# A sparse graph-attention layer: fewer count operations on VectorE, the edge one-hot scaled on ScalarE, the first search ahead of the arrival count's load

## What is computed

```python
h = relu(layernorm(x))
e = leaky_relu(h @ a[:256] + (h @ a[256:]).T, 0.2)      # 8192 x 8192
U = softmax(where(adj > 0, e, -9e15), axis=1)
prop = U @ h
rowsum = sum(U * 0.5 * U, axis=1)
feat = soft_threshold((1 - coe[2]) * h + prop - h * rowsum, 1e-6)
pu = U @ feat
feat_odd2 = coe[0] * (feat - coe[3] * pu) + (1 - coe[0]) * h0
feat_even2 = pu + (feat - coe[3] * pu) * rowsum
out = x + coe[1] * feat_even2 + (1 - coe[1]) * feat_odd2
```

## Time and profile before

| | us |
|---|---|
| median of 3 runs | 1553.82 |
| lowest and highest | 1546.98, 1554.12 |
| the profiled execution's own time | 1548.79 |
| its span | 1547.2 |

### The profile page before, as it was taken

The page is one execution under the profiler, slowest core; times in us unless marked ns, Lnnn a source line. Parts: engine busy times, 40 slices in busy tenths (PEclk is TensorE's granted clock), DMA queues, the critical chain, the costliest instruction groups (busy, mean ns, idle before and its releaser), DMA issues. The chain is left out here.

```text
span 1547.2 us, 27877 instructions
## 1 busy us (share of the span) xinstructions
PE 941.7 (61%) x3386; PEld 548.0 (35%) x3449; DVE 994.3 (64%) x5594; ACT 840.0 (54%) x1754; POOL 587.9 (38%) x642
## 2 busy tenths in 40 slices
PE   0013567687767666766766766767552555666676
PEld 0001124444444333333333333333331444544443
DVE  5882555787788788788788788788772112233444
ACT  2371456788777778777777777777422222111111
POOL 2000434534333233222122112112115777777776
PEclk9965568878888889888787777777655777788979
DMA  4974579889999999999999999988314556677887
GB/s 92 345 261 195 207 256 384 305 305 365 349 351 356 350 345 358 343 339 350 339 334 345 342 329 346 339 322 317 147 56 138 145 162 189 186 217 217 244 249 222
DMA packets 151067, 427.18 MB, mean 276 GB/s; under 512 B 30123, under 2 KB 112697, under 8 KB 134516
## 3 DMA queue, kind: packets, MB, share of 16 engines
q1 hardware_dynamic: 120872, 348.93, 61.0%
q0 software_dynamic: 30160, 77.90, 17.2%
HBM read 401.29 MB, written 33.85 MB: 281 GB/s over the span
## 5 line engine op out<-in xcount | busy, mean ns | idle before, releaser
L293 ACT ACTIVATE SG<-W,ABOVE 128x4096 bf16<-128x4096 f32 x126 | 467.0, 3706 | 120.0 <-DVE cnt L891 117.6
L586 POOL DMA_INDIRECT R<-haug_d,IDS x228 | 228.9, 1004 | 711.7 <-issue 711.7
L305 PE MATMUL TP<-SG,FOLD 128*128 128x512 bf16 x1006 | 315.3, 457 | 68.0 <-ACT SG L293 63.8
L628 ACT ACTIVATE DG<-ident,WSR 128x128 f32<-128x128 f32 x228 | 75.0, 391 | 311.3 <-PE ACC L642 284.9
L637 PE MATMUL ACC<-R,DG 128*128 128x256 f32 x538 | 193.1, 510 | 0.0
L1504 DVE SCALAR_TENSOR_TENSOR W<-ACC,SELF,W 128x256 f32<-128x256 f32 x63 | 30.5, 484 | 243.8 <-PE ACC L642 243.6
L305 PEld LDWEIGHTS TP<-SG,FOLD 128*128 128x128 bf16 x1008 | 117.0, 125 | 183.6 <-ACT SG L293 65.0
L636 PE MATMUL ACC<-XHO,ZB 128*128 128x256 bf16 x127 | 40.5, 319 | 220.6 <-ACTq L630 86.1
L637 PEld LDWEIGHTS ACC<-R,DG 128*128 128x128 f32 x538 | 125.7, 250 | 22.1 <-issue 0.5
L586 POOL DMA_INDIRECT R<-feat_d,IDR x115 | 110.4, 960 | 35.0 <-issue 33.5
L586 POOL DMA_INDIRECT W<-feat_d,IDR x113 | 108.6, 961 | 34.5 <-issue 32.6
(11 more groups left out here) (269 smaller groups left out, 2188.5 us busy)
## 6 DMA issues: line engine op xcount, KB each, us to landing
W<-in_adj_dram SPq DMA_DIRECT2D x128, 2048.0 KB, 9.0
haug_d<-R POOLq DMA_DIRECT2D x8, 1056.0 KB, 8.0
HTS<-haug_d SPq DMA_DIRECT2D x64, 132.0 KB
R<-in_x_dram SPq DMA_DIRECT2D x8, 1024.0 KB, 6.9
feat_d<-FTS SPq DMA_DIRECT2D x64, 128.0 KB, 2.0
W<-in_x_dram SPq DMA_DIRECT2D x64, 128.0 KB
W<-in_L_gnn_h_dram SPq DMA_DIRECT2D x64, 128.0 KB
W<-feat_d SPq DMA_DIRECT2D x64, 128.0 KB
```

The costliest lines, as they stand in the source:

```text
L293: nc.scalar.activation(SG[:, u, half(h)], W2[:, u, half(h)], ACT.Sign, scale=2.0 ** 100, bias=ABOVE[:], accum_out=DEG[:, u, h:h + 1]).then ...
L305: nc.tensor.matmul(KP[u], FOLD[:, b], SG[:, u, b * FW:(b + 1) * FW], start=False, stop=False)
L586: pool.indirect_dma_start(out=g[:, k, 0:w], out_offset=None, in_=table, in_offset=bass.IndirectOffsetOnAxis(ap=ids[:, k:k + 1], axis=0), * ...
L628: nc.scalar.mul(DG[:, u, k], ident[:], weights[:, k:k + 1])
```

## The change

1. `empty` (L1006), `base` (L1011) and the second step of `D` (L1023) go. What they gave is in constants: `NEGD`, `PIDX` and two comparisons are shifted by one, `want` takes the larger of itself and `HOLD` (made once), and the counting of slots weighs them with `SLOTW` (0 for the first, 1 for the next, 2 - KC for the last), so that it gives `D` at once. `FLG` is read from `SUMS`.
2. `RW` is made on ScalarE as `RT` times `WE`, behind the second half's signs. VectorE therefore waits for `rw_ready` of tile t-2 before it writes `RT` anew, and its `WE` moves behind the product of part C.
3. The first search stands ahead of the register load and the wait for the gathers; the second search stands ahead of part B's first step, and part B's other steps are spread anew among those of part A.

```diff
@@ constants, POOL and VectorE, once @@
+                nc.gpsimd.memset(SLOTW[:], 1.0)
...
+                nc.gpsimd.memset(SLOTW[:, 0:1], 0.0)
+                nc.gpsimd.memset(SLOTW[:, KC - 1:KC], float(2 - KC))
...
+                nc.vector.tensor_scalar(HOLD[:], SELF[:], -1.0, 1.0, ALU.mult, ALU.add)
@@ ScalarE, body @@
                     if ahead:
                         signs(act, t + 2, q + 1, u, 1)
+                    act.wait_ge(we_made, t - 1)
+                    nc.scalar.mul(RW[:, u], RT[:, u], WE[:, bass.ds(t - 1, 1)]).then_inc(rw_ready, 1)
                     weigh0(t - 1, q - 1 + u, 1 - u)
@@ VectorE, body @@
+                    if on:
+                        A_.mark(mx(FOUND[:, 0:8], KP[u]))
                     if on_b:
                         dve.wait_ge(gathered[ub], arrival_of(dve, tb + 1))
                         ts(M24[:], IOTAK, kb, G[:, ub, KR, COL_F2:COL_F2 + 1], ALU.is_equal, ALU.mult)
                         tt(U[:], G[:, ub, 0:KR, COL_F2], MASKD[:, ub], ALU.mult).then_inc(parts_ready, 1)
                     if on:
-                        A_.mark(mx(FOUND[:, 0:8], KP[u]))
                         A_.need()
                         dve.wait_ge(deg_taken, t + 1)
-                        tt(want, deg, SELF2[:, col], ALU.subtract)
+                        ts(want, deg, SELF2[:, col], HOLD[:, col], ALU.subtract, ALU.max)
                         swap(KB[:, 0], FOUND[:, 0:8], KP[u], EMPTY).then_inc(keys_taken[u], 1)
                         dve.wait_ge(keys_taken[u], q + 1)
                     if on_b:
+                        ts(SCR[:, ub, K:K + 1], SSELF[:, cb], 0.0, None, ALU.add)
+                    if on:
+                        A_.mark(mx(FOUND[:, 8:16], KB[:, 0]))
+                    if on_b:
                         dve.wait_ge(moved, tb + 1)
                         B_.mark(ts(scr, MOV[:, 0:K], F1[:, cb], None, ALU.add))
                     if on:
-                        A_.mark(mx(FOUND[:, 8:16], KB[:, 0]))
...
                     if on_b:
                         B_.need()
-                        ts(SCR[:, ub, K:K + 1], SSELF[:, cb], 0.0, None, ALU.add)
                         B_.mark(tt(scr, scr, PENM[:, ub], ALU.min))
...
-                    if on_b:
-                        dve.wait_ge(w_spread, tb + 1)
-                        stt(JNKW[:], IOTAK, kb, SPW, ALU.is_equal, ALU.mult, accum_out=WE[:, cb]).then_inc(we_made, 1)
                     if on:
                         A_.need()
                         A_.mark(tt(JK[:, 0, kk:2 * kk], JK[:, 0, kk:2 * kk], TWO[:, 0:kk], ALU.mult))
-                    if on_b:
-                        dve.wait_ge(we_made, tb + 1)
-                        ts(RW[:, ub], IOTA1[:], ROWE[:, cb], WE[:, cb], ALU.is_equal, ALU.mult).then_inc(rw_ready, 1)
...
                         C_.mark(stt(T0[:], ACCS[uc], invz, T0[:], ALU.mult, ALU.add))
+                    if on_b:
+                        dve.wait_ge(w_spread, tb + 1)
+                        stt(JNKW[:], IOTAK, kb, SPW, ALU.is_equal, ALU.mult, accum_out=WE[:, cb]).then_inc(we_made, 1)
...
-                        ts(empty, deg, float(-N), DENSE, ALU.is_equal, ALU.mult)
...
-                        stt(base, n, 1.0, empty, ALU.add, ALU.add)
                         A_(stt(neq, n, 2.0, want, ALU.mult, ALU.not_equal))
-                        A_.mark(stt(n_all, neq, DENSE, base, ALU.mult, ALU.add))
+                        A_.mark(stt(n_all, neq, DENSE, n, ALU.mult, ALU.add))
...
-                        A_(stt(JNKD[:], SUMS[:, 0:KC], float(P), ONES_K[:, 0:KC], ALU.is_gt, ALU.mult, accum_out=over))
-                        A_(stt(D, over, float(KC), over, ALU.is_lt, ALU.mult))
-                        A_.mark(ts(CTL[0:1, col, 0], D[0:1], 1.0, None, ALU.max))
+                        A_(stt(JNKD[:], SUMS[:, 0:KC], float(P), SLOTW[:], ALU.is_gt, ALU.mult, accum_out=D))
+                        A_.mark(ts(CTL[0:1, col, 0], D[0:1], 1.0, None, ALU.add))
...
+                        if on_b:
+                            dve.wait_ge(rw_ready, tb + 1)
                         ts(RT[:, u], IOTA1[:], ROWE[:, col], None, ALU.is_equal)
```

More of the change, by code:

```diff
@@ L30, in adj_preln_kernel @@
     KG = 4
+    KC0 = KR + 2
     RING = 4
@@ L84, in adj_preln_kernel @@
         SELF2 = sb("SELF2", [P, NT])
+        HOLD = sb("HOLD", [P, NT])
+        SLOTW = sb("SLOTW", [P, KC0])
         SSELF = sb("SSELF", [P, NT])
@@ L877, in body @@
                     kk = K if isinstance(t, int) and t < HEAD else KL
-                    per = 30 + 4 * (kk > 16)
-                    A_ = Steps(dve, s1_step, t * 34 if kk > 16 else t * 30 + 4 * HEAD, per)
+                    per = 29 + 4 * (kk > 16)
+                    A_ = Steps(dve, s1_step, t * 33 if kk > 16 else t * 29 + 4 * HEAD, per)
                     B_, C_ = (Steps(dve, s_, t_ * n_, n_) for s_, t_, n_ in ((s2_step, tb, 4), (s3_step, tc, 7)))
@@ L883, in body @@
                     cb, cc = bass.ds(tb + 1, 1), bass.ds(tc + 1, 1)
-                    deg, want, empty, n, neq, base, n_all, D, pre, left, end, over = (cnt[:, i:i + 1] for i in range(12))
+                    deg, want, n, neq, n_all, D, pre, left, end = (cnt[:, i:i + 1] for i in range(9))
                     invz, q_z, coef = (s[:, i:i + 1] for i in range(4, 7))
@@ L906, in body @@
                     if on:
-                        A_.mark(mx(FOUND[:, 8:16], KB[:, 0]))
                         A_.need()
+                        if kk > 16:
+                            A_.mark(swap(KB[:, 1], FOUND[:, 8:16], KB[:, 0], EMPTY))
+                            A_.need()
                     if on_b:
@@ L930, in body @@
                         B_.need()
[L931 removed]
+                        B_.mark(tt(scr, scr, PENM[:, ub], ALU.min))
                     if on:
@@ L935, in body @@
                         A_.mark(ts(KS[:, 0:kk], KI[:, 0:kk], 9, None, ALU.arith_shift_right))
+                    if on_b:
+                        B_.need()
+                        B_.mark(nc.vector.reduce_max(m[:, 0:1], SCR[:, ub], AX.X))
                     if on_c:
@@ L942, in body @@
                         A_.mark(ts(CODES[:, 0:kk], KS[:, 0:kk], 2.0 ** (NB - 1), None, ALU.add))
+                    if on_b:
+                        B_.need()
+                        nc.vector.tensor_scalar_mul(m[:, 1:2], m[:, 0:1], -1.0).then_inc(top_ready, 1)
                     if on_c:
@@ L1021, in body @@
                         dve.wait_ge(sums_made, t + 1)
-                        A_(stt(JNKD[:], SUMS[:, 0:KC], float(P), ONES_K[:, 0:KC], ALU.is_gt, ALU.mult, accum_out=over))
-                        A_(stt(D, over, float(KC), over, ALU.is_lt, ALU.mult))
-                        A_.mark(ts(CTL[0:1, col, 0], D[0:1], 1.0, None, ALU.max))
-                        A_.mark(stt(JNKP[:], IOTAE[:, 0:KC], D, SUMS[:, KC:2 * KC], ALU.is_equal, ALU.mult, accum_out=pre))
-                        ts(FLG[0:1, col], over[0:1], float(KC), None, ALU.is_equal)
+                        A_(stt(JNKD[:], SUMS[:, 0:KC], float(P), SLOTW[:], ALU.is_gt, ALU.mult, accum_out=D))
+                        A_.mark(ts(CTL[0:1, col, 0], D[0:1], 1.0, None, ALU.add))
+                        A_.mark(stt(JNKP[:, 0:KC - 1], IOTAE[:, 0:KC - 1], D, SUMS[:, KC + 1:2 * KC], ALU.is_equal, ALU.mult, accum_out=pre))
+                        ts(FLG[0:1, col], SUMS[0:1, KC - 1:KC], float(P), None, ALU.is_gt)
                         A_.mark(ts(left, n_all, D, 0.0, ALU.subtract, ALU.max))
@@ L1034, in body @@
                         stt(RE[:, u], IOTAE[:], end, AGE[:], ALU.is_lt, ALU.mult).then_inc(edges_ready, 1)
-                        A_.mark(stt(kcc[:, u:u + 1], D[0:1], 1.0, kcc[:, u:u + 1], ALU.max, ALU.add))
-                        ts(MASKD[:, u], IOTA1[:, 0:KR], D, None, ALU.is_lt)
+                        A_.mark(stt(kcc[:, u:u + 1], D[0:1], 1.0, kcc[:, u:u + 1], ALU.add, ALU.add))
+                        ts(MASKD[:, u], IOTAE[:, 0:KR], D, None, ALU.is_lt)
                         A_.need()
```

17 lines of the change are left out of this document (4 added, 13 removed).

## The result

| | before | changed |
|---|---|---|
| median of 4 runs, us | 1551.03 | 1488.89 |
| lowest and highest | 1546.98, 1554.12 | 1487.16, 1496.91 |
| the profiled execution's own time | 1548.79 | 1490.07 |
| its span | 1547.2 | 1488.4 |

The ratio is 0.961 [0.957, 0.966]: faster, by 62 us. The forecast was 88 us faster (1465), with the range up to 1503. So the direction and the range held, and the gain fell 26 us short of the forecast's.

What follows compares the result with a forecast made beforehand. VectorE's in-order chain was taken to set the 14.54 us period. Terms 0.70 + 0.48 + 0.18 + 0.30 - 0.05 = 1.61 us, with 0.1 allowed, gave 13.0 us a tile, 88 us in all: 1465 us, own range 1440 to 1492, widened to 1503.

Steps and rivals of the forecast that it cites:

- The bound: Middle stage's 63 tiles: VectorE's body of in-order operations sets the 14.54 us period; ScalarE waits 2.2 us a tile for it.
- the 0.3 I had given: Sign of being right: ScalarE's wait for VectorE's count operation falls from 2.2 us a tile to 0.3 or less.
- The register load: From L891 to the swap L901: the load runs beside the first search, gain 0.70 us a tile, bounds 0.1 and 0.9.
- The rival that the load waits for the search's end: Register load starts only after the search; first gain falls from 0.70 to 0.1, kernel 1500 us; chance 0.09.
- The order of the scores: From second search to L948: alternating steps of parts A and B find inputs complete, gain 0.48 us, bounds 0.2 and 0.6.
- The rival by which only removed work counts (1478): New order fills no gaps; only removed operations and 0.47 us idle time go, 1.33 us a tile; chance 0.09.
- RW and WE: From L965 to L981: 0.81 us becomes 0.40, WE costs 0.23 in its new place; gain 0.18 us, bounds 0 and 0.35.
- The counts: Removing three VectorE count operations (L1006, L1011, L1023) gains 0.30 us a tile, bounds 0.2 and 0.47.
- the allowance: 0.1 us a tile for DMA, ScalarE and VectorE limits ending almost together; period taken as 13.0 us, gain 1.53.
- My 0.05 for `rw_ready`: VectorE's RT waits for ScalarE's RW, with 0.7 us of cover; 0.05 us a tile taken off the gain.
- The DMA engines as a flat limit: Rival: by DMA share the period stays at 13.8 us, gain 0.74, kernel 1511 us; chance 0.10.
- RT's wait for ScalarE's RW: Slower rival: RW comes later than RT's turn by more than was gained; 1581 us at 2.8 us later; chance 0.02.

Runs made afterwards that it cites:

- the early start: Changed kernel, but POOL reads the tile's number of slots before its wait for the product that frees the buffer: 1477.71 us, ratio 0.952.
- The two edits together: Changed kernel with adj loads in DMAs of 1024 columns and the slots read ahead of POOL's wait: 1466.82 us, ratio 0.945.

## Why the prediction was right, and where it was short

**The bound** was right: VectorE's chain of in-order operations set the period of the kernel before. The kernel before with less `adj` shows that the DMA engines didn't, 14.58 us with them at 0.76, and ScalarE waited for VectorE. In the changed kernel ScalarE still waits 1.1 us a tile, more than the 0.3 I had given, because VectorE's period stayed longer.

**The register load** was right in its mechanism and nearly in its size: M24 at 0.68 us in one body and 0.83 in the other, forecast 0.70, and 0.62 us gained of 0.70 where no gather is waited for. The rival that the load waits for the search's end fell. With the load first again the "issue" wait came back, and the kernel took about 0.3 us a tile more.

**The order of the scores** was right, 0.50 us against 0.48. The operations on VectorE that need nothing of each other do start 0.07 to 0.10 us apart, which is less than the 0.15 to 0.20 they last. By the sentence of the Trainium skill that I had gone by ("VectorE: DVE Perf Modes", "The DRAIN you can't avoid": the next operation does not start until the pipe is empty) this term would have been nothing; the trace disagrees here as it did before. The same section adds that a next operation that is not held starts earlier, which I had left out; that fits these rows. This is a reading of pieces: no kernel had the old order of the scores alone. The rival by which only removed work counts (1478) lies nearer to the result than my own number, but for another reason: the reorderings did arrive, and other waits took time back.

**RW and WE** was a wrong term. I had 0.18 us, from two dependent steps of 0.2 between L965 and L981. The trace has L976 to L986 at 0.64 us: the wait of the second step is followed by register steps and another wait before the product can start, 0.42 us from L980 to L986 and not 0.2. WE costs 0.16 behind the second product. The balance of the pieces is about nothing. The run that undid this part shows that it is worth 22 us all the same, 16 of them through the wait for TensorE that it keeps away. My way of costing, one part at a time on the trace of before, can't see that.

**The counts** were about right: 0.19 us in their stretch where I had 0.24, and 0.20 in the pieces of the kernel that took them back. What they are worth in the total stays open.

**The step that failed** is the allowance: "With three limits so near each other and tiles that differ, I allow 0.1 us", with "The gathers (POOL busy 26% of the stretch) have room" behind it. POOL had room, but POOL's busy time says nothing of when a gather lands. Both changed-kernel profiles have 0.35 to 0.41 us a tile of waiting for gathers or for TensorE at the two places L905 and L1028, where the one before had 0.14. With less `adj` the gathers' part was gone, which shows that they land late because of the bulk load beside them. With smaller pieces of the same bytes it was 2.4 us, with those and the early start 1.3, where the two profiles of the changed kernel have 12.9 and 5.3; the early start alone shows it ahead of tile 12 only. That the gathers take their turn behind the bulk load's long packets is how I read this; it is argued, not shown. The two edits together win 20 us, of which only 6.6 lie in the 46 tiles; of the 0.42 us a tile that were missing, they explain 0.14 to 0.23 (against the one profile and the other). The rest is the RW term, 0.2, and the wait for TensorE's sums. That wait goes with stretches in which TensorE's granted clock is low, as shown above; my sum had no term for it. What lowers the clock stays open. My 0.05 for `rw_ready` has nothing to show for it in these tiles: RT never waited there.

**The rivals.** The DMA engines as a flat limit at 13.8 us and 1511 fell: the same engines went on to 13.09 us a tile. So did the lower limit that I had taken from the Trainium skill ("HBM Reference", first table), 358 GB/s and 1519 us; here 372 to 381 GB/s stood over 609 us. I had read the figure wrongly as a limit for this case: the text under that table gives it for two cores that stream at once, and says that a core alone goes well above it. RT's wait for ScalarE's RW, the mechanism on the other side, has no row among VectorE's waits from 391 to 1000 us, and 1.6 us in two tiles ahead of them.

**Luck.** The result lies 3 us inside my own range (to 1492), and neither the gathers nor TensorE's clock, which took part of the gain, stood among my rivals. The direction rests on the mechanism; that the range held owes something to luck.

## What to carry to other kernels

When a chain of in-order operations gets shorter, look at every wait in it that had just been met: TensorE's spread came in time by 0.6 us before and would be late now that the chain ahead of WE is 1.1 us shorter. So a part of a change can be worth more beside the others than its pieces say. When transfers with a deadline share DMA engines with bulk loads, try smaller pieces of the bulk load: splitting 16 KB a row into 4 KB took about 15 us off this kernel, of which 4 to 8 us lie in the 46 tiles where the gathers had been late, and most of the rest ahead of the first tile, for a reason that I didn't follow. A wait that moves from one execution to the next, as the gathers' did from 12.9 to 5.3 us, needs more than one profile. Before costing a step, count what the sequencer has to do behind its wait: here the register load behind a running search hardly showed, while the register steps and the second wait behind L980 stood in a gap of 0.42 us where a plain dependent pair takes 0.2.

## What the runs showed of the hardware

- A register load of VectorE's sequencer runs beside an operation in the engine: with a search of 0.69 us in front, M24 started 0.61 us behind the search's start, so nothing of the load was left to be seen; in the other body it started 0.76 us behind it.
- The DMA engines moved 381 GB/s over 609 us at a share of 1.02, more than in the kernel before in its steady stretch (344 GB/s) and close to the 388 GB/s that it reached over 42 us.
- TensorE's granted clock changes within a tile, and VectorE feels it: eight products took 3.22 us at 0.55 and 1.99 at 1.00, and all 43 waits of 0.5 us or more for the sums behind them fell where it was 0.50 to 0.65.
- Two chips ran the same kernel at 1551 and at 1740 us. In the changed kernels on the slower chip, waits stood at other lines than on the faster one, so its pieces can't be laid beside those of another chip.
